# An RWKV time mix with a mixture of experts on one core: one weight block requested earlier, the key weights' low half built on GpSimd, and the third key product issued one place earlier

## The reference, cut to what matters

```
shifted = pad(hidden)[:, :-1]
key   = hidden * mix_k + shifted * (1 - mix_k)     # value, rec alike with mix_v, mix_r
k = key @ Wk ; v = value @ Wv ; r = sigmoid(rec @ Wr)
scan over t:  mfo = max(mx, k+tf); out = (e^(mx-mfo) num + e^(k+tf-mfo) v) / (e^(mx-mfo) den + e^(k+tf-mfo))
              mfs = max(mx+td, k); num = e^(mx+td-mfs) num + e^(k-mfs) v; den = ... ; mx = mfs
x = layernorm(x + (r * out) @ Wo)
x = layernorm(x + moe(x))          # 8 experts of width 16, top 2
```

## Time and profile before

| | |
|---|---|
| Median of 3 runs | 473.17 us (472.75 to 473.2) |
| Profiled execution, its own time | 473.77 us |
| Its span in the trace | 471.9 us |
| Busy share of the span | PE 96%, DVE 88%, ACT 75%, POOL 64% |
| Granted TensorE clock, mean | 0.996 of full |

### The profile page before, as it was taken

One profiled execution on the slowest core, in us unless ns is written; L12 is line 12 of the kernel. 1 busy time (PEld: TensorE's weight loads), 2 busy tenths in 40 slices (PEclk: granted clock), 3 DMA queues, 4 the chain that ended last, 5 costly groups with the idle time before them and its releaser, 6 DMA issues. The chain is left out here.

```text
span 471.9 us, 6614 instructions
## 1 busy us (share of the span) xinstructions
PE 454.0 (96%) x1962; PEld 334.8 (71%) x1962; DVE 416.2 (88%) x620; ACT 354.7 (75%) x800; POOL 301.5 (64%) x287
## 2 busy tenths in 40 slices
PE   8999899999999999999999999999999999999993
PEld 3444566667888777877778777887778777878751
DVE  5999988899989979999899998999799997875866
ACT  1667666867787689876888778876898769768685
POOL 2354776489637987369846698279873696434335
PEclk9999999999999999999999999999999999999998
DMA  9603220023000042000420031200420012400015
GB/s 245 204 0 115 89 89 1 1 93 110 1 1 0 2 156 90 24 0 30 152 90 0 0 135 67 69 0 1 157 90 22 0 47 69 156 0 1 0 47 222
DMA packets 20100, 30.38 MB, mean 64 GB/s; under 512 B 2016, under 2 KB 7136, under 8 KB 20064
## 3 DMA queue, kind: packets, MB, share of 16 engines
q1 hardware_dynamic: 20064, 29.95, 19.4%
HBM read 21.56 MB, written 8.39 MB: 63 GB/s over the span
## 5 line engine op out<-in xcount | busy, mean ns | idle before, releaser
L560 ACT ACTIVATE PR<-PR 128x512 f32<-128x512 f32 x128 | 74.3, 581 | 29.3 <-DVE PR L858 14.9
L1150 POOL TENSOR_SCALAR NM<-SUM,RS 128x1 f32<-128x1 f32 x30 | 8.1, 271 | 106.5 <-ACT RS L560 106.5
L1144 POOL TENSOR_TENSOR DQ<-DEN,EX 128x512 f32<-128x512 f32 x32 | 41.9, 1309 | 22.2 <-DVE DEN L829 22.2
L883 DVE SCALAR_TENSOR_TENSOR KT<-D,VEC,XT 128x512 f32<-128x512 f32 x57 | 53.9, 983 | 1.2 <-POOL KL L1122 1.2
L313 PE MATMUL PV<-VH,WVH 128*128 128x512 f32 x112 | 47.7, 426 | 2.0 <-DVE NU L853 2.0
L313 PE MATMUL PK<-KH,WKH 128*128 128x512 f32 x112 | 48.1, 429 | 0.0
L317 PE MATMUL PR<-RL,WRH 128*128 128x512 f32 x112 | 45.0, 402 | 1.2 <-POOL RL L1122 1.1
L313 PE MATMUL PR<-RH,WRH 128*128 128x512 f32 x112 | 45.0, 402 | 0.8 <-POOL WRL L1175 0.6
L829 DVE TENSOR_TENSOR_SCAN DEN<-PK,EX 128x512 f32<-128x512 f32 x32 | 39.0, 1219 | 7.6 <-ACT EX L560 5.7
L317 PE MATMUL PV<-VL,WVH 128*128 128x512 f32 x112 | 44.1, 394 | 0.5 <-POOL VL L1122 0.5
L560 ACT ACTIVATE EX<-PK 128x512 f32<-128x512 f32 x32 | 19.1, 597 | 33.5 <-DVE PK L822 33.5
(11 more groups left out here) (249 smaller groups left out, 1269.1 us busy)
## 6 DMA issues: line engine op xcount, KB each, us to landing
XT<-in_xt SPq DMA_DIRECT2D x32, 256.0 KB, 3.5
XN<-in_x SPq DMA_DIRECT2D x28, 256.0 KB, 2.7
out<-XN SPq DMA_DIRECT2D x28, 256.0 KB, 2.0
X1T<-in_wo SPq DMA_DIRECT2D x1, 1024.0 KB, 5.1
XT<-in_x SPq DMA_DIRECT2D x4, 256.0 KB, 4.2
out<-XT SPq DMA_DIRECT2D x4, 256.0 KB, 2.5
X1T<-in_wk SPq DMA_DIRECT2D x2, 256.0 KB, 5.2
XN<-in_wv SPq DMA_DIRECT2D x2, 256.0 KB, 5.5
```

What stands on the lines that cost most here:

```text
L560: eng.activation(*a, **k).then_inc(q[s], 1)
L883: eng.scalar_tensor_tensor(out=full(b, which, c), in0=D[:, c, :], scalar=VEC[:, 2 + which, c:c + 1], in1=XT[:, c, 0:T], op0=ALU.mult, op1= ...
L1144: eng.tensor_tensor(DQ[:, :], DEN[:, 0:T], EX[:, 1, :], ALU.add).then_inc(q["e"], 1)
L1150: eng.tensor_scalar(NM1[:, col(t)], total, RS1[:, col(t)], scale, ALU.mult, ALU.mult)\
```

## The change

Three edits, which touch four queues.

1. Sync: the first piece of the key weights (256 KB, `s_ws00`) is issued directly behind the first input chunk, and in front of the other three chunks.
2. The low half of the key weights is made by GpSimd in four 128x512 instructions, two in slot 0 and two in slot 1 in front of the value weights' four. VectorE's 128x2048 instruction is gone. The semaphore `s_lwk` counts to 4, and those who wait for it (Sync in front of the Wo load, TensorE in front of the split key products) wait accordingly.
3. TensorE: key product 2 stands in slot 0 behind receptance product 0, in front of value product 1.

```diff
             eng.dma_start(VEC[:, :, :], vec).then_inc(q["vec"], 16)
-            for c in range(C):
+            load_xt(0, 0)
+            load_w(X1T, wk, "ws00", 0, 128)
+            for c in range(1, C):
                 load_xt(0, c)
             for i, (lo, hi) in enumerate(((0, 128), (128, 256), (256, H))):
-                load_w(X1T, wk, f"ws0{i}", lo, hi)
+                if i:
+                    load_w(X1T, wk, f"ws0{i}", lo, hi)
...
-            eng.wait_ge(q["lwk"], 1)
+            eng.wait_ge(q["lwk"], C)
...
-                    eng.wait_ge(q[("lwk", "lwv", "lwr")[which]], j + 1 if which else 1)
+                    eng.wait_ge(q[("lwk", "lwv", "lwr")[which]], j + 1)
...
-                if 0 < s < U - 1:
+                if 1 < s < U - 1:
                     key(s + 1)
                 if s == C:
                     project(0)
                 rec(s)
+                if s == 0:
+                    key(2)
...
-            def low_weights():
-                eng.wait_ge(q["hw"], 1)
-                eng.tensor_tensor(WKL[:, :, :], X1T[:, :, :], WKH[:, :, :].bitcast(F32), ALU.subtract)\
-                   .then_inc(q["lwk"], 1)
...
-                if s == 0:
-                    low_weights()
...
             def low_weights(i, *blocks):
-                stage, high, low, done = ((XN[0], WVH, WVL, "lwv"), (XN[1], WRH, WRL, "lwr"))[i - 1]
+                stage, high, low, done = ((X1T, WKH, WKL, "lwk"), (XN[0], WVH, WVL, "lwv"), (XN[1], WRH, WRL, "lwr"))[i]
...
+                if s == 0:
+                    low_weights(0, 0, 1)
                 if s == 1:
+                    low_weights(0, 2, 3)
                     low_weights(1, *range(C))
```

## The result

| | before | changed |
|---|---|---|
| Median | 473.12 us (6 runs, 472.75 to 473.2) | 476.05 us (6 runs, 475.45 to 476.42) |
| Ratio, 95% interval | | 1.0061, 1.0048 to 1.0074 |
| Profiled execution, own time | 473.77 us | 476.42 us |
| Span | 471.9 us | 474.6 us |

The change makes the kernel 2.9 us slower, where +1.5 us was forecast and 475.7 us was the upper end of the range. The sign and the dearest single cause, worth 1.5 us, were right. A second cause of about 0.8 us had been costed at nothing. The remaining 0.6 us did not come again when the changed kernel ran a second time, and stays unexplained.

What follows compares the result with a forecast made beforehand. Bounds: TensorE's queue at the start, a VectorE-ScalarE ring from 22.8 to 55.7 us, TensorE from 120 to 420. Terms 0 + 1.5 + 0 + 0 = +1.5 gave 475.3 for the profiled execution, 474.7 us as median; range 473.2 to 475.7.

Steps and rivals of the forecast that it cites:

- the dearest single cause: Slot 1: VectorE's three key mixes meet GpSimd's value-weight subtractions, which the added work moves back; +1.5 us.
- A second cause: Kernel start: the three other input chunks land 0.9 us later behind the first key piece; cost 0, from 0 to 0.9.
- The low half on GpSimd: Slots 0 and 1: four added GpSimd instructions delay VectorE's key mixes in slot 1; +1.5 us, bounds +0.1 and +2.3.
- the turn: From 22.8 to 55.7 us: one round from VectorE through ScalarE and back, 10.47 us between successive `scan_den` starts.
- The step model: Slot 1: pairs each mix with one GpSimd instruction by start offset; +1.98 us on VectorE, 0.46 into slack, +1.5 through.
- VectorE's freed 2.28 us: Before `scan_den(1)`: the removed VectorE instruction's time becomes idle, since `scan_den(1)` still waits for ScalarE; gain 0.
- the moved key product: TensorE, slot 0: key product 2 before value product 1 only moves the gap to value product 2; gain 0.
- The early request: Kernel start: the first key piece lands at 5 instead of 7.6 us, input chunks 0.9 later; gain 0, cost 0.
- a cover of about 1 us: Kernel start: TensorE's queue, held until 8.21 us, and VectorE's 1.20 us wait before the first scan hide late chunks.
- the input chunks are late: Rival, kernel start: TensorE waits for JUNK, +0.9 on top of 1.5, 475.6 us; chance 0.11.
- The upper bound of the forecast: Kernel start: if TensorE were ready earlier than in the profiled execution, the chunks' whole 0.9 us delay would show.
- Gain 0: Kernel start: TensorE is held by its own queue until 8.21 us, so key weights landing earlier bring nothing.

Runs made afterwards that it cites:

- request back: The changed kernel with the old Sync order, first key piece behind all four input chunks; 475.15 us, ratio 1.0029 to the kernel before.
- lows alone: The kernel before with only the key weights' low half moved to GpSimd, two instructions each in slots 0 and 1; 475.12 us, ratio 1.0032.
- all in slot 1: The changed kernel with the old Sync order and all four key subtractions in slot 1, before the value weights' four; 475.05 us, ratio 1.0031.
- request alone: The kernel before with only the Sync order changed, first key piece directly behind the first input chunk; 474.38 us, ratio 1.0022.
- request back and all key subtractions in slot 0: The changed kernel with the old Sync order and all four key subtractions on GpSimd in slot 0; 473.18 us, ratio 0.9998.
- three and one: The changed kernel with the old Sync order, three key subtractions in slot 0 and one in slot 1; 473.70 us, ratio 1.0009.
- The changed kernel again: The changed kernel, unaltered, run once more beside the kernel before; 475.81 us, ratio 1.0049.

## Why the prediction was wrong, point by point

**The low half on GpSimd: right, by its own steps.** The mixes were forecast at about 1.0, 1.7 and 1.7 us and measured at 0.98, 1.77 and 1.78. `scan_den(2)` was forecast +1.5 and measured +1.51 in the turn. The other profiles confirm it: the turn is 11.96 to 11.99 us in the five where three mixes meet GpSimd (both profiles of the changed kernel, request back, lows alone, all in slot 1), and 10.46 to 10.47 in the eight where only the first does, as before. Nothing behind it gave the time back: of each profile's span, take off the start of the first scan, what the turn has over 10.47, and 0.6 us where the clock falls, and 459.3 to 460.3 us are left in all 14. The step model was too sure of the pairing, as the run with one subtraction in slot 1 shows (2.26 us for one mix instead of 1.0 and 1.76). That mix started 0.84 us into a GpSimd instruction, and the first mix of "request back" did so too and took 0.99; what decides between the two was not found.

One reading behind this term doesn't hold. The prediction took line 870 at 0.69 us as an operation that GpSimd leaves alone, but GpSimd was idle there, from 36.18 to 40.41. Rows beside GpSimd's WVL stream, which begins at 31.17, do show it for operations with an input in PSUM. VectorE before, 31 to 35 us:

```profile
32.59 0.69 DVE L853 TENSOR_TENSOR NU<-NUM,PV 128x512 f32<-128x512 f32 x1
33.20 1.22 DVE L816 TENSOR_TENSOR_SCAN M<-CST,PK 128x512 f32<-128x512 f32 x1
```

**VectorE's freed 2.28 us and the moved key product: right, worth nothing.** The first became a wait of 2.23 us, the second a wait in another place.

**The early request: wrong.** This is the step that failed: "it uses up a cover of about 1 us" and "Cost 0". It was the rival "the input chunks are late", with a chance of 0.11. Two terms of it were mis-sized, the lateness and the cover.

- The lateness of chunk 1 was taken as one transfer's 0.9 us. The first difference was at 7.12, 5.75, 5.94 and 6.35 us in the four profiles with the request behind the first chunk, 6.29 on average, against 4.68 to 5.15 (4.88 on average) in the eight with the old order: 1.4 us on average, and 2.2 once. The key piece itself landed at 5.0 to 5.3 us in all four, so what varies is the time from there to chunk 1.
- The cover was one execution's. TensorE's weight load for the first key product stood at 8.21 us in the profile that the forecast read, and elsewhere with the old order between 7.5 and 8.4, because the zeros' matmuls end between 7.6 and 9.0. The first scan, 12.28 us in the profile before, is at 11.86 on average over the eight profiles with the old order (11.34 to 12.49), and at 12.45 with the early request (11.89 to 13.27): 0.6 in the profiles, and 0.6 to 1.5 in the times of the request alone. Medians with and without the request give 0.73 where all key subtractions are in slot 0, 0.75 on the kernel before, and 0.80 on the changed kernel, hence "about 0.8".
- Behind the early request VectorE's own chain sets the scan: it starts 6.14 to 6.20 us behind the first difference in all four profiles and never waits for TensorE, while with the old order it waits for TensorE in seven of eight. The upper bound of the forecast (0.9 "if TensorE were ready earlier") had the mechanism, but was left as a rival and not weighed into the sum.
- "Gain 0" was one execution's reading too: in three of the eight profiles with the old order the load for the first key product waits for the key piece, as below. An early request would bring this load forward there. Behind the first chunk that is worth nothing, since the first scan then waits for VectorE. Where the queue is free early, the late chunks set the first key product: at its first matmul in the first profile of the changed kernel (0.99 us of wait for RW), at JUNK in that of the request alone.

The weight load in "request back" (0.81 us of idle time where 0.24 is usual; 0.46 in "request back and all key subtractions in slot 0" and 0.73 in "three and one"):

```profile
7.60 0.30 PEld L299 LDWEIGHTS PK<-RW,X1T 128*128 128x128 f32 x2 [0.81 <-DMA X1T<-in_wk]
```

**The sum.** 1.5 + 0 + 0 + 0 should have read 1.5 + about 0.8. The changed kernel again, at +2.3, is that. The +2.9 of the first result lies above it by 0.6; the two intervals overlap (1.0048 to 1.0074 and 1.0034 to 1.0063). The fall of the clock doesn't explain it: three of its six executions have a mean clock of 0.995 to 0.997, as only profiles without the fall have, and they took 475.45 to 476.23 us, like the other three. Whether it is chance stays open. The range ended at +2.6 because the late chunks were held to be unlikely.

**The page's rule.** The Trainium skill's "SBUF — State Buffer", section "SBUF: two separate sides", names whole-instruction exclusion. Its direction is borne out (one mix let two GpSimd instructions by in full), its price here is less than a full sum: about 1.7 us for a pair (mixes at 37.60 and GpSimd's instructions at 37.10 and 38.77 in the changed profile) and not 2.04.

## What to carry to other kernels

Moving work to an engine with idle time is not free where it slides other work of that engine against VectorE operations with two SBUF inputs: look at who stands beside whom after the move, and count the meetings. A transfer that is issued earlier makes the transfers that it passes later, here by 1.4 us on average and 2.2 once, where the input chunks land about 1 us apart; pass only those whose data is needed last. A cover that is read from one profile at the start of a kernel, before the clock has risen, is one draw of several: take its lower end.

## What the runs showed that had not been expected

- When they meet in a stream, GpSimd's subtractions go from 1.24 us apart to 1.67, and VectorE's two-input operation from 0.74 to 1.78 us: both engines pay, VectorE more (1.04 against 0.43 us).
- A mix that starts late in a GpSimd instruction can be passed over twice: 2.26 us (one of 14 profiles).
- The zeros' matmuls are 0.85 us apart until somewhere between 4.9 and 7.6 us, and 0.43 afterwards, in the same code: the moment at which TensorE's clock rises is not fixed by the program.
- A fall of the granted clock to 0.50 for 3.4 us behind a wait of 1.96 to 1.97 us, in six of 14 profiles; eight matmuls added into that wait brought nothing.
